# Longer vector products in a CIN tower: groups of 4, 4, 3 and 2 tiles in place of pairs

## The reference

```
for W in (W0, W1, W2):                                  # xk = x0 at first, then 64 maps
    xk = relu(einsum('bmd,bhd,mhk->bkd', x0, xk, W))
    outs.append(sum(xk, axis=2))
z = concatenate(outs, axis=1)                           # (1024, 192)
h = relu(concatenate([z, dense_ctx]) @ W_top1 + b_top1)
h = relu(h @ W_top2 + b_top2)
y = h @ W_top3
```

## Time and profile before

| what | before |
|---|---|
| median of 3 runs | 644.31 us (643.63 to 645.4) |
| the profiled execution | 642.9 us, its span 641.1 us |
| VectorE busy | 558.1 us (87%), 346 instructions |
| TensorE busy | 559.1 us (87%), 2440 matmuls |
| GpSimd busy | 488.4 us (76%) |
| ScalarE busy | 224.6 us (35%) |
| DMA | 150.94 MB, mean 235 GB/s |
| granted TensorE clock | 0.997 of full |

### The profile page before, as it was taken

One profiled execution on the slowest core, in us unless ns is written; L12 is line 12 of the kernel. 1 busy time (PEld: TensorE's weight loads), 2 busy tenths in 40 slices (PEclk: granted clock), 3 DMA queues, 4 the chain that ended last, 5 costly groups with the idle time before them and its releaser, 6 DMA issues.

```text
span 641.1 us, 6648 instructions
## 1 busy us (share of the span) xinstructions
PE 559.1 (87%) x2440; PEld 179.6 (28%) x2440; DVE 558.1 (87%) x346; ACT 224.6 (35%) x351; POOL 488.4 (76%) x364
## 2 busy tenths in 40 slices
PE   0047998999999998999999899999899999989998
PEld 0012232332323232323232232222232233323342
DVE  0047998999999999999999999999999999898810
ACT  0032607053341616160524425161606143340422
POOL 6756798879888888978788888888797979675500
PEclk9998999999999999999999999999999999999999
DMA  3298857677876758676778778675767687772000
GB/s 104 45 384 299 305 189 291 242 297 266 305 271 246 272 206 297 235 288 222 294 267 298 267 260 288 225 280 214 294 232 282 253 300 265 295 268 72 1 0 0
DMA packets 52835, 150.94 MB, mean 235 GB/s; under 512 B 9697, under 2 KB 17377, under 8 KB 52802
## 3 DMA queue, kind: packets, MB, share of 16 engines
q1 hardware_dynamic: 44610, 148.40, 62.8%
q0 software_dynamic: 8192, 2.11, 2.5%
HBM read 147.33 MB, written 3.15 MB: 235 GB/s over the span
## 4 chain that ended last, share of the span: by engine, by line
DVE 47%; DMA 16%; PE 15%; issue 13%; POOL 7%; SPq 2%; ACT 0%; DVEq 0%; POOLq 0%
DVE prod L286 43%; DMA x0bc<-x_rows 12%; PE y_ps L413 10%; POOL emb L247 6%; DVE z L314 4%; PE x0g_ps L473 2%; DMA x_rows<-emb 2%; DMA emb<-table,row_sb 2%; SPq L214 1%; PE x_ps L473 1%; POOL pool_prod L260 1%; PE x0g_ps L466 1%; PE x0g_ps L467 1%; PE x_ps L467 1%; PE x_ps L466 1%
## 5 line engine op out<-in xcount | busy, mean ns | idle before, releaser
L286 DVE TENSOR_TENSOR prod<-x0bc,x_ps 128x2048 f32<-128x2048 f32 (+1 forms) x252 | 456.2, 1879 | 8.6 <-ACT x_ps L370 7.2
L413 PE MATMUL y_ps<-prod,w_sb 128*64 128x512 f32 x1640 | 383.2, 597 | 36.6 <-DVE prod L286 36.6
L247 POOL DMA_INDIRECT emb<-table,row_sb x256 | 245.0, 957 | 65.4 <-issue 63.4
L260 POOL TENSOR_TENSOR pool_prod<-x0bc,x_sb 128x1024 f32<-128x1024 f32 x102 | 242.3, 2381 | 50.4 <-ACT x_sb L379 39.3
L413 PEld LDWEIGHTS y_ps<-prod,w_sb 128*64 128x64 f32 x1640 | 115.2, 137 | 287.3 <-issue 225.4
L413 PE MATMUL y_ps<-pool_prod,w_sb 128*64 128x512 f32 x408 | 105.1, 595 | 5.1 <-POOL pool_prod L260 5.1
L370 ACT ACTIVATE x_ps<-y_ps 64x512 f32<-64x512 f32 x128 | 73.0, 570 | 87.8 <-PE y_ps L413 85.2
L286 DVE TENSOR_TENSOR prod<-x0bc,x0g_ps 128x2048 f32<-128x2048 f32 x32 | 72.3, 2281 | 34.6 <-DMA x0bc<-x_rows 31.0
L379 ACT ACTIVATE x_sb<-relu 64x512 f32<-64x512 f32 x128 | 80.4, 628 | 3.4
L374 ACT ACTIVATE relu<-y_ps 128x512 f32<-128x512 f32 x48 | 28.7, 597 | 147.1 <-PE y_ps L413 146.3
L355 ACT ACTIVATE x0g_ps<-x0g 128x1024 f32<-128x1024 f32 x16 | 16.4, 1028 | 156.9 <-DMA x0g<-x_rows 156.9
(11 more groups left out here) (27 smaller groups left out, 45.4 us busy)
## 6 DMA issues: line engine op xcount, KB each, us to landing
x0bc<-x_rows SPq DMA_DIRECT2D x256, 512.0 KB, 6.6
x0g<-x_rows SPq DMA_DIRECT2D x16, 512.0 KB, 4.7
emb<-table,row_sb POOLq DMA_INDIRECT x256, 5.0
x_rows<-emb SPq DMA_DIRECT2D x16, 128.0 KB, 2.1
w_sb<-w SPq DMA_DIRECT2D x2, 512.0 KB, 4.5
x_rows<-emb SPq DMA_DIRECT2D x16, 64.0 KB, 2.0
x0bc<-wt SPq DMA_DIRECT2D x1, 512.0 KB, 5.3
x0bc<-wt_a SPq DMA_DIRECT2D x1, 256.0 KB, 4.0
```

The costliest lines, as they stand in the source:

```text
L247: pool.indirect_dma_start(emb[:, turn, DIM * n:DIM * (n + 1)], None, table, bass.IndirectOffsetOnAxis(row_sb[:, at:at + 1], 0)).then_inc(g ...
L260: pool.tensor_tensor(pool_prod[:, n % POOL_RING, :], x0bc[:, slot(s, j), :], x[:], ALU.mult).then_inc(pool_products, 1)
L286: made = dve.tensor_tensor(prod[:, n % RING, 0:count, cols], tiles[:, :, cols], right.unsqueeze(1).to_broadcast([P, count, right.shape[1]] ...
L413: made = pe.matmul(ps[MAPS * h:MAPS * (h + 1), :], w, moving[:, HALF * h:HALF * (h + 1)], start=first, stop=final)
```

## The change

VectorE's groups no longer have a fixed size. `SIZES` gives the sizes of a layer by its number of tiles: 13 tiles are groups of 4, 4, 3 and 2, 12 are 4, 4, 2 and 2, 11 are 4, 4, 2 and 1, and layer 0 is one group of 4. The first group of layers 1 and 2 is still made in two halves, now of 4 x 512 elements. `prod` counts in tiles, 12 of them; `places` gives each group consecutive tiles and the number of the last earlier group that used any of them. `POOL_BEFORE` says anew between which groups TensorE takes GpSimd's tiles. VectorE and SyncE wait for or release by the new groups; `bc_in` still counts pairs.

```diff
-GROUP = 2
+PAIRED = 2
+
+SIZES = {4: [4], 11: [4, 4, 2, 1], 12: [4, 4, 2, 2], 13: [4, 4, 3, 2]}
-RING = 4
+
+RING = 12
-POOL_BEFORE = {3: [2, 3, 5], 4: [2, 3, 4, 5], 5: [2, 3, 4, 5, 5]}
+POOL_BEFORE = {3: [1, 2, 3], 4: [1, 2, 3, 3], 5: [1, 2, 2, 3, 3]}
...
 def groups_of(s, l):
-    tiles = list(range(TILES - POOL_COUNT[s][l - 1])) if l else list(range(LOW))
-    return [tiles[i:i + GROUP] for i in range(0, len(tiles), GROUP)]
+    sizes = SIZES[TILES - POOL_COUNT[s][l - 1] if l else LOW]
+    return [list(range(sum(sizes[:g]), sum(sizes[:g + 1]))) for g in range(len(sizes))]
...
+def places():
+
+    found = []
+    for x in STAGES:
+        for group in groups_of(*x):
+            first = found[-1][1] if found else 0
+            if first + len(group) > RING:
+                first = 0
+            end = first + len(group)
+            shared = [m for m, (a, b, _) in enumerate(found) if a < end and first < b]
+            found.append((first, end, shared[-1] + 1 if shared else 0))
+    return found
...
-        prod = sb("prod", [P, RING, GROUP, PAIR])
+        prod = sb("prod", [P, RING, PAIR])
...
-                    sp.wait_ge(products, before((s, 2)) + j // GROUP + 1)
+                    group = next(g for g, tiles in enumerate(groups_of(s, 2)) if j in tiles)
+                    sp.wait_ge(products, before((s, 2)) + group + 1)
...
+            def wait_tiles(s, group):
+                for pair in sorted({j // PAIRED for j in group}):
+                    dve.wait_ge(bc_in[pair], 32 * (s + 1))
+
+            def product(n, tiles, x, h=None):
+
+                first, end, free = PLACES[n]
+                if free > 0 and h != 1:
+                    dve.wait_ge(products_used, free)
...
                 for g, group in enumerate(groups_of(s, 0)):
-                    dve.wait_ge(bc_in[g], 32 * (s + 1))
+                    wait_tiles(s, group)
                     at = slot(s, group[0])
-                    product(before((s, 0)) + g, GROUP, x0bc[:, at:at + GROUP, :], x0g_ps)
+                    product(before((s, 0)) + g, x0bc[:, at:at + len(group), :], x0g_ps)
...
                     for i, t in enumerate(group):
-                        made = contract(ps, w[:, t, :], prod[:, n % RING, i, :], g == i == 0,
+                        made = contract(ps, w[:, t, :], prod[:, PLACES[n][0] + i, :], g == i == 0,
                                         last and i == len(group) - 1)
                     made.then_inc(products_used, 1)
```

More of the change, by code:

```diff
@@ L72, in after @@
     return before(x) + len(groups_of(*x))
+def places():
[9 more added lines that the diff above has]
+    return found
+PLACES = places()
 def pool_before(x):
@@ L157, in cin_tower_kernel @@
         x0g_in = sem("x0g_in")
-        bc_in = [sem(f"bc_in{g}") for g in range(TILES // GROUP)]
+        bc_in = [sem(f"bc_in{g}") for g in range(TILES // PAIRED)]
         w0_ready = sem("w0_ready")
@@ L213, in load_tiles @@
                     rows = x0_rows[SHIFT[j]:SHIFT[j] + FIELDS, cols].unsqueeze(1).to_broadcast([FIELDS, QUART, PAIR])
-                    sp.dma_start(x0bc[:, slot(s, j), :], rows).then_inc(bc_in[j // GROUP], 16)
+                    sp.dma_start(x0bc[:, slot(s, j), :], rows).then_inc(bc_in[j // PAIRED], 16)
             sp.dma_start(ids_sb[:], ids).then_inc(ids_in, 16)
@@ L255, in layer @@
                 for k, j in enumerate(pool_tiles(s, l)):
-                    pool.wait_ge(bc_in[j // GROUP], 32 * (s + 1))
+                    pool.wait_ge(bc_in[j // PAIRED], 32 * (s + 1))
                     n = pool_before((s, l)) + k
@@ L279, in _ @@
         def _(dve):
-            def product(n, count, tiles, x, h=None):
-                if n >= RING and h != 1:
-                    dve.wait_ge(products_used, n - RING + 1)
+            def wait_tiles(s, group):
[5 more added lines that the diff above has]
+                    dve.wait_ge(products_used, free)
                 cols = slice(0, PAIR) if h is None else slice(HALF * h, HALF * (h + 1))
                 right = x[:].rearrange("p h c -> p (h c)")[:, cols]
-                made = dve.tensor_tensor(prod[:, n % RING, 0:count, cols], tiles[:, :, cols],
-                                         right.unsqueeze(1).to_broadcast([P, count, right.shape[1]]), ALU.mult)
+                made = dve.tensor_tensor(prod[:, first:end, cols], tiles[:, :, cols],
+                                         right.unsqueeze(1).to_broadcast([P, end - first, right.shape[1]]), ALU.mult)
                 if h != 0:
@@ L307, in layer @@
                             dve.wait_ge(spread_done[l - 1], 4 * s + 2 * h + 2)
-                            product(n, count, tiles, x, h)
+                            product(n, tiles, x, h)
                     else:
-                        product(n, count, tiles, x)
+                        product(n, tiles, x)
             def sums(s, l):
@@ L433, in layer0 @@
                     for i, t in enumerate(group):
-                        made = contract(ps, w0s_sb[:, t, :], prod[:, n % RING, i, :], False, t == LOW - 1)
+                        made = contract(ps, w0s_sb[:, t, :], prod[:, PLACES[n][0] + i, :], False, t == LOW - 1)
                     made.then_inc(products_used, 1)
```

## The result

The changed kernel takes 695.52 us (median of 4, 693.72 to 696.12), the kernel before 644.86 beside it; the ratio is 1.0785 with a 95% interval of 1.0762 to 1.0808. It is slower, as forecast, but by 51 us and not by 33: the time lies 5.5 us above the range. The profiled execution took 693.72 us with a span of 691.9.

The account below looks back on a forecast made before the run. VectorE sets the pace, with a transfer chain almost as long. Periods of 37.4 us put layer 0 of step 15 33 us later; with +1.7 behind it, about 35 on 642.9 gave 678, stated as 677; range 659 to 690.

Parts of the forecast that it names:

- the late maps: ScalarE's start in layer 1: 18.5 us after the layer's start where it was 16.9, +1.65 us, passed on to GpSimd.
- the late burst: Loads of tiles 8 to 15: the last lands about 19.4 us into layer (s, 2), where it was 17.3.
- What f is: Time from last gather to its stores' issue: between 2.2 and 6.6 us, taken as the gathers' median, 3.8.
- The slope from steps 9 and 6: Stores' delay per us the last tile lands later behind the last gather: 0.6, giving 4.0 us.
- w: Wait for the fourth tile before layer 0 in each step: 2.9 us, bounds 2.1 and 4.3.
- From store to layer 0: Stores to fourth tile 12.96 us, plus 0.07 until VectorE's product in layer 0.
- The fourth tile of step 2 hangs on nothing that changes: Start of the kernel: loads hold GpSimd's first pass, so layer 0 of step 2 starts at 102.7 us, not 99.57.
- The tail: After layer 0 of step 15: TensorE starts layer (14, 2) later, +1.7 us.
- B: Transfers don't collide, last gather to stores stays 2.2 us: 667 to 669 us; chance 0.2.
- C: TensorE's late start does not reach the gathers, only the wait for four tiles stays: 657 us; chance 0.08.
- D: Fourth tile is in whenever VectorE comes, only the saved 7.0 us count: 636 to 638 us; chance 0.05.
- E: Gathers near their upper bound, or stores queue behind the last tile: up to 696 us; chance 0.09.

Follow-up runs that it names:

- l1_pairs: The changed kernel with layer 1 back in pairs, layer 0 in one group of 4 and layer 2 in long groups; 686.61 us.
- l2_pairs: The changed kernel with layer 2 back in pairs, layer 0 in one group of 4 and layer 1 in long groups; 681.75 us.
- l0_pairs: The changed kernel with layer 0 back in two pairs; 665.78 us.
- l0_four_only: The changed kernel with layers 1 and 2 back in pairs, only layer 0 in one group of 4; 670.50 us.
- half_burst: The changed kernel loading only half the bytes of tiles 8 to 15 from step 3 on, so computing with stale halves; 676.59 us.
- first_pairs: The changed kernel with two pairs in the very first layer 0 (step 0) alone; 693.12 us.
- gathers_early: The changed kernel with the last four gathers of a step moved into layer (s, 1); 663.23 us.

## Why the prediction was wrong, point by point

**The mechanism held.** The saving is 108 instructions and 7.0 us. TensorE, the maps, GpSimd's start and last gather, and the release of the loads came where the text put them. The waits went where it put them, before layer 0. l1_pairs and l2_pairs show that both parts of the chain, the late maps and the late burst, cost; l0_pairs and l0_four_only that the four tiles at once do.

**The step that failed is "What f is": 3.8 was taken, 5.1 was measured.** Cut the stretch from layer (s, 1) to layer 0 of step s+2 into the pieces of the prediction. In the mean of steps 2 to 12 they are 18.67 (maps) + 5.67 + 13.38 + 5.06 (f) + 13.59 (store to layer 0) = 56.37; the prediction had 18.5 + 5.7 + 13.4 + 3.8 + 13.0 = 54.4. Of the 2.0 us, 1.3 are f. They are shared by two periods: 38.35 for 37.4, over 13 periods 12.4 us, of which f is 8.

The median of the six gathers was the wrong reading. In order of issue they landed after 6.6, 5.1, 4.2, 3.4, 2.9 and 2.2 us, and when the last of them was issued, at 331.80, the last tile of the burst was 1.3 us from its landing. A last gather deeper in the burst is like the slow ones of that row, and half_burst shows that it is the burst. The slope from steps 9 and 6, which gave 4.0, was too low as well. The measured w, 3.8, lies between the 2.9 that was taken and the bound of 4.3.

The size of f alone would not have left the range: with f = 5.1 the prediction's own sum gives w = 3.55, a period of 38.0 and 686 us. The start, below, puts 4 us on that, and the next term 3.6.

**From store to layer 0** it took 13.6 and not 13.0. Between the stores and the read of x0 behind them lie 3.06 us in the mean, where the kernel before has 2.73; half_burst has 2.62, so these 0.3 go with the burst too. The fourth tile's load took 0.15 longer, and the product starts 0.22 us behind its landing where 0.07 was taken; these two stay open.

**The start: "The fourth tile of step 2 hangs on nothing that changes" was false.** Layer 0 of step 2 started at 106.74, not at 102.7: 4.0 us. TensorE's timeline at the start of the changed kernel, and ScalarE's:

```profile
43.48 6.52 PE L441 MATMUL y_ps<-prod,w0s_sb 128*64 128x512 f32 x16 [5.89 <-DVE prod L314]
55.87 5.44 PE L441 MATMUL y_ps<-prod,w_sb 128*64 128x512 f32 x16 [5.88 <-DVE prod L314]
```

```profile
71.67 2.35 ACT L398 ACTIVATE x_ps<-y_ps 64x512 f32<-64x512 f32 x4 [9.49 <-PE y_ps L441]
```

Before, TensorE's matmuls of layer 0 began at 38.52, those of (0, 1) at 47.87, and the maps of (0, 1) came at 67.93. I had looked at GpSimd's first product, which a load held, and had not followed TensorE, which stands idle twice for a first group of four; from there GpSimd's next layer and the last gather of step 2 are late by the same 3.7 us (90.71 for 86.98). first_pairs brings the maps back, and shows that most of it is lost again on the way to layer 0.

**The tail** cost 86.6 - 85.35 = 1.25 us for 1.7 that were forecast (691.9 - 605.30 against 641.1 - 555.75). Together: 12.4 + 4.0 - 0.45 = 16, and the profiled execution took 693.7 where the sum had 678.

**The rivals.** B needs f = 2.2 and C a GpSimd that is not late; both are refuted by the rows of step 5. D, that only the saved work counts, is refuted by the idle time before layer 0. E, with 0.09, had f near 6.6, which did not come; that the time fell near its 696 us all the same is luck, since the start and the way from store to layer 0 made up for the smaller f. The range was closed at 690 because the upper part of E was held to be rare; no run had shown f so deep in a burst, so there was no ground for that.

## What to carry to other kernels

A longer instruction saves its fixed cost, here 0.065 us, only on the engine that runs it; it delays by its added length whoever waits for its first part and whoever waits for its last read: the consumer, the slot that is to be reloaded, and what is queued behind that load. Where several chains are as long as the bound within 1 us, price each of them, and close them into a loop: a wait in front of layer 0 also shifted the loads that lengthened the wait. When a small transfer moves into a burst of large ones, take its duration from such transfers that lay wholly inside one, not from the median.

## What the runs showed of the hardware

A gather of 128 rows whose stores followed after 2.2 us at the end of a burst took 6.1 us in the middle of one (gathers_early), with the same number of bytes. Half the bytes in the burst, in as many packets, brought it back to 2.4 us (half_burst). That contention was expected, its size was not.

TensorE's granted clock fell in 11 of the 14 layers 0 from step 2 on in the changed kernel: their 16 matmuls took 5.0 to 5.4 us, after TensorE had stood idle for the long group. In steps 3, 12 and 13 they took 3.65, after idle times of 2.6 to 2.9 us, as long as some of those before a fall (2.3 to 4.4), so the idle time alone does not say when it falls. Timeline of TensorE (layer 0 of step 6) and busy times of step 5 and of 4 us in it (PE, PEld, DVE, ACT, POOL, clock, DMA):

```profile
264.46 5.26 PE L441 MATMUL y_ps<-prod,w0s_sb 128*64 128x512 f32 x16 [2.92 <-DVE prod L314]
```

```profile
242.11:280.29 38.18, 34.02 (x150) 12.37 (x148) 34.56 (x15) 13.38 (x21) 29.54 (x23) 0.96 0.68 244
262.00:266.00 4.00, 1.54 (x4) 0.54 (x6) 4.00 (x4) 3.85 (x7) 1.65 (x2) 0.79 0.59 218
```

Part of those 4 us is at the lower of the two levels, 1.2 for 2.4 GHz; 16 matmuls took 5.26 us for 3.65 in layer (5, 1). The Trainium skill, "TensorE: Matmul & The Clock Gate", section "Part 1: The HAM clock gate (the "warmup" mystery)", says that the clock follows how busy the array has been; the trace agrees in so far as the falls from step 2 on came at a layer 0 that TensorE had waited for, but for one, 2.4 us behind the matmuls of layer 0 of step 3. In the steady state it cost next to nothing: the maps of layer 1 came 18.61 us after the start of the layer in ten of the steps 2 to 12, whether or not the clock had fallen in the layer 0 before, and 19.26 us in step 3. What it cost at the start was not tried apart.
